# exp(-z) by ScalarE's Ln and Exp in place of VectorE's reciprocal, and another opening, in a fused attention and MLP kernel

## The reference

```
s = clip(hs @ Ws1.T @ Ws2.T + bs2, -32, 32)        # (B, H, T, M)
z = cumlogsumexp(s, axis=t);  es = exp(s);  enz = exp(-z)
A = tril(q @ k.T) * scale                           # q, k with rotary positions
ok = enz * (A @ es)
qv = softmax(ok)
W2 = tril((qv * enz) @ es.T)
o = rmsnorm(W2 @ v) * g_norm_weight * silu(g)
x = x + o @ Wo.T + mlp(hs)
```

## Time and profile before

| what | value |
|---|---|
| time, median of 3 runs | 1154.71 us (1154.1 to 1155.89) |
| profiled execution: time, span | 1155.05 us, 1153.3 us |
| busy TensorE | 1110.0 us, 96% of the span |
| busy VectorE | 950.5 us, 82% |
| busy ScalarE | 640.7 us, 56% |
| busy POOL | 422.4 us, 37% |
| mean granted TensorE clock | 0.986 |

### The profile page before, as it was taken

The page is one execution under the profiler, slowest core; times in us unless marked ns, Lnnn a source line. Parts: engine busy times, 40 slices in busy tenths (PEclk is TensorE's granted clock), DMA queues, the critical chain, the costliest instruction groups (busy, mean ns, idle before and its releaser), DMA issues.

```text
span 1153.3 us, 19874 instructions
## 1 busy us (share of the span) xinstructions
PE 1110.0 (96%) x6872; PEld 937.2 (81%) x6872; DVE 950.5 (82%) x1815; ACT 640.7 (56%) x1750; POOL 422.4 (37%) x307
## 2 busy tenths in 40 slices
PE   5789999999999999999999999999999999999995
PEld 4568888888888888888888888888888888888885
DVE  5978888788888889888887888878888888888863
ACT  4455456555645556554656655565564565655442
POOL 4323244422434335232453324443252434523131
PEclk9889999999999999999999999999999999999997
DMA  4002000020002000020000200001000100000001
GB/s 161 1 1 75 2 1 1 1 76 1 2 1 76 1 1 2 1 76 1 1 1 1 75 1 1 1 11 65 1 1 2 75 2 1 2 1 19 1 19 38
DMA packets 9124, 23.03 MB, mean 20 GB/s; under 512 B 832, under 2 KB 5824, under 8 KB 8000
## 3 DMA queue, kind: packets, MB, share of 16 engines
q1 hardware_dynamic: 9024, 21.76, 5.2%
HBM read 19.66 MB, written 2.10 MB: 19 GB/s over the span
## 4 chain that ended last, share of the span: by engine, by line
PE 82%; DVE 5%; issue 3%; ACT 2%; POOL 1%; POOLq 0%; DVEq 0%; ACTq 0%
PE bank L205 20%; PE bank L207 18%; PE bank L206 18%; PE bank L298 4%; PE bank L330 3%; PE bank L311 3%; PE bank L355 3%; PE bank L344 2%; PE bank L347 2%; PE bank L346 2%; PE bank L300 2%; DVE og L808 1%; PE bank L502 1%; PE bank L314 1%; PE bank L322 1%
## 5 line engine op out<-in xcount | busy, mean ns | idle before, releaser
L1165 POOL TENSOR_TENSOR inter_lo<-ffb,inter_hi 128x512 fp32r<-128x512 f32 x64 | 83.5, 1329 | 417.2 <-ACT inter_hi L650 417.2
L1156 POOL TENSOR_TENSOR qkT<-ra,xs 128x512 f32<-128x512 f32 x128 | 164.5, 1285 | 109.3 <-DVE xs L899 77.2
L619 ACT ACTIVATE sm<-bank,mx 128x64 f32<-128x64 f32 x256 | 76.5, 325 | 148.4 <-DVE mx L855 148.4
L896 DVE TENSOR_TENSOR ra<-bank,rope 128x512 f32<-128x512 f32 x128 | 87.8, 686 | 48.3 <-ACT xs L601 47.2
L844 DVE RECIPROCAL enzT<-enzT 128x256 f32<-128x256 f32 x64 | 111.6, 1744 | 0.0
L899 DVE TENSOR_TENSOR xs<-xs,rope 128x512 f32<-128x512 f32 x128 | 111.0, 867 | 0.0
L205 PE MATMUL bank<-xh,wqk_hi 128*128 128x512 f32 x256 | 110.7, 432 | 0.0
L205 PE MATMUL bank<-xh,wgu_hi 128*128 128x512 f32 x256 | 106.2, 415 | 0.0
L624 ACT ACTIVATE At<-bank 128x128 f32<-128x128 f32 x128 | 35.4, 276 | 126.7 <-DVE At L779 126.6
L207 PE MATMUL bank<-xh,wqk_lo 128*128 128x512 f32 x256 | 102.1, 399 | 0.0
L207 PE MATMUL bank<-xh,wgu_lo 128*128 128x512 f32 x256 | 101.5, 396 | 0.0
(11 more groups left out here) (146 smaller groups left out, 3171.6 us busy)
## 6 DMA issues: line engine op xcount, KB each, us to landing
raw<-in_w_qkvg SPq DMA_DIRECT2D x8, 1024.0 KB, 5.1
scaled<-in_w_scaled SPq DMA_DIRECT2D x8, 640.0 KB, 7.4
packed<-in_w_packed SPq DMA_DIRECT2D x8, 384.0 KB, 5.6
acc<-in_x SPq DMA_DIRECT2D x4, 512.0 KB, 8.0
out<-acc SPq DMA_DIRECT2D x3, 512.0 KB, 2.9
out<-acc SPq DMA_DIRECT2D x2, 256.0 KB, 2.1
ws_raw<-in_w_slot SPq DMA_DIRECT2D x8, 48.0 KB, 1.8
rope<-in_rope_tab SPq DMA_DIRECT2D x1, 256.0 KB, 5.8
```

Of the source, the lines that this page charges most:

```text
L619: ins = act.activation(sm[:, c], src[:, c], ACT.Exp, bias=mx[:, g:g + 1], accum_out=ssum[:, g:g + 1])
L896: dve.tensor_tensor(two(ra[i % 2][:, :]), two(pj[i][:, :]), cos, ALU.mult).then_inc(cos_done, 1)
L1156: pool.tensor_tensor(qkT[:, i, :], ra[i % 2][:, :], xs[i % 2][:, :], ALU.add).then_inc(roped, 1)
L1165: pool.tensor_tensor(inter[1][e][:, :], ffb[e][:, :], inter[0][e][:, :].bitcast(F32), ALU.subtract).then_inc(inter_lo, 1)
```

## The change

exp(-z) is now computed on ScalarE in two activations over all 512 tokens, Ln and then Exp with scale -1, and the reciprocals are gone from VectorE. The opening is ordered anew: 24 matmuls of the identity ahead of everything on TensorE (`WARM`), the VG weights loaded and split in two parts, other load order; VG projection ahead of the inner slot product; block 1's second half of x, its inner product and the slot scores moved into stage 0; and one block of x prepared in each of stages 0 (block 2) and 1 (block 3), where `prep` is set, through one PSUM bank (`sc[0]`). `normalise` is split into `x_stats` and `x_scale`. A new SBUF tile `xb` holds the scaled x of blocks 2 and 3, the Ws1 parts have tiles of their own, and the reserved DMA scratch is set to 1024.

```diff
@@ ScalarE
+            def invert(n, par):
+                act.wait_ge(scan_done, 2 * n + 2)
+                act.activation(enzT[par][:, :], enzT[par][:, :], ACT.Ln).then_inc(z_done, 1)
+                act.wait_ge(z_done, n + 1)
+                act.activation(enzT[par][:, :], enzT[par][:, :], ACT.Exp, scale=-1.0).then_inc(enz_ready, 1)
...
+                if first:
+                    copy_J(0, rg[0][:, :])
+                    invert(0, 0)
                 if not last:
                     slot_exp(st + 1, npar)
...
+                if prep:
+                    x_hi(prep, 0, sc[0])
+                    x_hi(prep, 1, sc[0])
                 if bp == 3 and more:
                     split_hi(hp + 1, W_QK)
                     prepare_scales(hp + 1)
...
+                else:
+                    invert(st + 1, npar)
                 softmax_exp(st)
@@ VectorE
-            def invert(n, par, b):
-                dve.wait_ge(scan_done, 2 * n + b + 1)
-                c = slice(b * T, (b + 1) * T)
-                dve.reciprocal(enzT[par][:, c], enzT[par][:, c]).then_inc(enz_ready, 1)
...
                 gate_arg(st, 1)
+                if prep:
+                    x_stats(prep)
...
                 hidden(st, 1)
+                if prep:
+                    x_scale(prep)
...
                 softmax_in(st, par)
-                if not last:
-                    invert(st + 1, npar, 0)
+                if prep:
+                    x_lo(prep, 0, sc[0])
                 softmax_max(st)
+                if prep:
+                    x_lo(prep, 1, sc[0])
...
                 if not last:
-                    invert(st + 1, npar, 1)
                     gate_g(st + 1, npar, 2)
@@ TensorE, opening
+            pe.wait_ge(ident_set, 1)
+            for i in range(WARM):
+                pe.matmul(pj[3][:, 0:P], ident[:, :], ident[:, :], start=True, stop=True)
+            for k in range(KT):
+                transpose_x(0, k, rg[k])
+            for i in range(NT):
...
             pe.wait_ge(ws1_lo, 1)
-            slot_inner(0, sc[0])
+            slot_inner(0, rg[0])
             project_qk(0, 0, 0, 0)
             project_qk(0, 0, 0, 1)
+            transpose_x(1, 0, rg[1])
             project_qk(0, 0, 0, 2)
-            slot_inner(1, rg[0])
             project_qk(0, 0, 0, 3)
@@ TensorE, stage
                 slot_reads(st)
+                if prep:
+                    pe.wait_ge(clip_done, st + 2)
+                    transpose_x(prep, 0, sc[0])
                 if not first:
                     outputs(st, 0, php, None)
                 if not last:
                     project_vg(st + 1, nbp, nhp, 2, True)
                 slot_rows(st)
+                if prep:
+                    x_split(KT * prep + 1)
+                    transpose_x(prep, 1, sc[0])
@@ POOL, opening
             x_pow(0)
+            pool.wait_ge(xn_done, 1)
+            for k in range(KT):
+                pool.wait_ge(w_hi if k else vg0_hi, 1)
+                pool.tensor_tensor(wvg[1][:, k, :], raw_k[:, k, 512:1024], wvg[0][:, k, :].bitcast(F32),
+                                   ALU.subtract).then_inc(w_lo if k else vg0_lo, 1)
+            split_lo(0, W_QK)
             pool.wait_ge(ws1_hi, 1)
...
+            dequantise(0, W_GU)
             x_pow(1)
-            split_lo(0, W_QK)
-            dequantise(0, W_GU)
```

More of the change, by code:

```diff
@@ L55 @@
 SLOT_K = 3 * GROUP
+WARM = 24
 W_VG, W_QK, W_GU, W_OD = range(4)
@@ L173, in build @@
         xn = [og[:, :].rearrange("p (n d) -> p n d", n=NT), G[1][:, :].rearrange("p (n d) -> p n d", n=NT),
[L174 removed]
+              xb[:, :, :], xb[:, :, :]]
         ws1 = osq[:, 0:KT * P].rearrange("p (k n) -> p k n", k=KT)
[L176 removed]
         xhl = (xh, xl)
@@ L495, in stage @@
                 pe.wait_ge(p_ready, st + 1)
[L496 to L499, removed]
+                if not first:
                     pe.wait_ge(acc_done, 2 * st - 1)
@@ L505, in stage @@
                     project_qk(st + 1, nbp, nhp, 0)
+                if prep:
+                    slot_inner(prep, sc[0])
+                if not last:
                     project_qk(st + 1, nbp, nhp, 1)
@@ L527, in stage @@
                 pe.wait_ge(v_ready, 4 * st + 4)
-                if first:
-                    slot_inner(3, rg[1])
-                else:
+                if not first:
                     pe.wait_ge(acc_done, 2 * st)
                 values(st, bp, 0)
[L533 to L536, removed]
+                if not last:
                     pe.wait_ge(J_ready, st + 2)
@@ L650, in hidden_hi, with x_hi @@
                 act.activation(inter[0][e][:, :], ffb[e][:, :], ACT.Copy).then_inc(inter_hi, 1)
[L652 to L655, removed]
+            def x_hi(bp, k, src):
+                act.wait_ge(xT_full, KT * bp + k + 1)
+                act.activation(xh[:, k, tokens(bp)], src[:, :], ACT.Copy).then_inc(xh_done, 1)
             def inner_copy(bp, src):
@@ L667, in _ @@
             ins.then_inc(ws1_hi, 1)
[L668 to L673, removed]
             prepare_scales(0)
@@ L698, in stage @@
                 more = hp < HP - 1
+                prep = st + 2 if st < 2 else None
+                if first:
+                    gate_square(st, 0)
                 off_diagonal(*a_args, 0, SCALE)
                 off_diagonal(*a_args, 1, SCALE)
-                gate_square(st, 0)
+                if not first:
+                    gate_square(st, 0)
                 gate_tanh(st, 0)
+                if first:
+                    slot_exp(0, 0)
+                    inner_copy(1, rg[1])
                 if bp == 1:
@@ L737, in stage @@
                     swap_halves(st + 1, 0)
+                if prep:
+                    inner_copy(prep, sc[0])
+                if not last:
                     swap_halves(st + 1, 1)
@@ L747, in stage @@
                     swap_halves(st + 1, 2)
-                if first:
-                    x_hi(3)
                 off_diagonal(*w_args, 2, 1.0)
@@ L1000, in stage @@
                 if first:
-                    invert(0, 0, 1)
-                if not first:
+                    gate_gelu(st, 0)
+                    inner_lo(1, rg[1])
+                else:
                     gate_scale(st)
@@ L1205, in stage @@
                 more = hp < HP - 1
+                if not first:
+                    norm_pow(st)
                 if first:
                     x_pow(2)
-                else:
-                    norm_pow(st)
                 if bp == 1:
```

254 lines of the change are left out of this document (130 added, 124 removed).

## The result

The changed kernel takes 1171.59 us (median of four runs, 1170.55 to 1173.59), the kernel before 1155.2 on the same occasions (four runs, 1154.1 to 1155.89). The ratio is 1.0144, 95% interval 1.0132 to 1.0155: slower by 1.4%, or by 16.4 us. 1180 was forecast, with 1157 to 1200 as the range. The profiled execution took 1171.61 us with a span of 1169.9, 16.6 above that of before.

What follows compares the result with a forecast made beforehand. TensorE, busy 1110.0 of 1153.3 us, was taken as the bound. Turns with clock falls 22.0, opening -7.5 and stage 1 +11.1 sum to +25.6; 1155.05 + 25.6 - 0.34 gives 1180 us, range 1157 to 1200.

Steps and rivals of the forecast that it cites:

- The turns: Seven turn stages (bp 3): the call makes the softmax 2.74 us late, TensorE waits 1.93 each, 13.5 us in all.
- The clock after such a wait: After the turns' TensorE waits: clock falls five times of seven, costing 8.5 us, bounds 0 and 11.9.
- likeliest range: Range of the likeliest case: 1164 us (no falls, opening 5 better) to 1190 (all falls, opening 6 worse).
- Ordinary stages: 22 ordinary stages: the call fits in ScalarE's wait for the maximum, ending 2.0 us before the softmax; cost 0.
- The opening: Start to stage 1's scores: scores start at 78.3 instead of 85.79, gain 7.5 us, bounds 2 and 13.
- The walk: Step-by-step timing of the new opening from row durations, from x's scaling at 7.95 to stage 1's scores at 78.3.
- The gap near 22: Opening: TensorE idles 6.7 us before block 1's transposes, waiting for x scaled behind decode, gates and a POOL-held sine product.
- Stage 1: Stage 1 now prepares block 3's x: idles of 2.4 and 2.7 us, two clock falls; cost 11.1, bounds 7 and 13.
- The end: The end of the kernel: claimed to be untouched by the change, with no term in the sum.
- A switch costs twice its row: Rival: table switches cost double, a call takes 6.5 us, turns wait 4.5 each; +54.7, 1209 us, chance 0.12.
- The loads cost nothing: Rival: both loads run in waits, a call takes 1.3 us, turns lose nothing; -3.3, 1151 us, chance 0.11.
- The turns absorb the call: Rival: ScalarE's lateness in the turns is caught up, only the opening counts; +3.6, 1158 us, chance 0.08.

Runs made afterwards that it cites:

- e2_call_alone: The kernel before with only exp(-z) changed: Ln and Exp on ScalarE ahead of the softmax, no reciprocals on VectorE; 1167.16 us, ratio 1.0094.
- e3_no_loads: The changed kernel with Copy in place of Ln, leaving one table load in the trace; 1151.65 us, ratio 0.996.
- e4_turns: The changed kernel with the exp(-z) call moved ahead of prepare_out in the seven turn stages; 1158.76 us, ratio 1.0028.
- e9_longer_wait: The changed kernel with one more 512-column copy on ScalarE ahead of the call in each turn stage; 1187.79 us, one run.
- e1_opening_alone: The changed kernel with exp(-z) back on VectorE as two reciprocals a stage; 1153.7 us, ratio 0.9987.
- e10_opening_dve: The same opening as e7_opening, but with exp(-z) by VectorE's reciprocals; 1147.66 us, ratio 0.9933.
- e7_opening: The changed kernel, call ahead of prepare_out (turns) and second x copy (stages 0, 1), opening reordered to scale block 1's x earlier; 1146.43 us, ratio 0.9922.

## Why the prediction was right, and where it was off

The forecast difference was 25.6 us, the measured one 16.4. The measured time lies well inside the range, but most of the distance is one term.

**The turns: right.** Predicted 1.93 us of lateness seven times, 13.5 in all; measured 1.92 a stage, 13.4 over the seven. The softmax was to be 2.74 late and is 2.65. e2_call_alone shows that the call alone does it, e3_no_loads that its loads do, e4_turns that its place does. The call, predicted at 3.9, delays the softmax by 3.78.

**The clock after such a wait: the step that failed.** "1.93 lies between; I take five falls of seven: 8.5 us" became no fall of seven and 0 us, the lower bound I had named. The lateness of 1.93 shows as an idle of 1.70, closer to the 1.43 of the earlier trace rows that had kept 1.00 than to the 2.59 that had not. In e9_longer_wait idles of 2.20 to 2.22 us brought a fall six times in seven, at 1.6 us each. Without that term the sum is 1171.8, 0.2 from the measured median, and a difference of 17.1 against 16.4. Part of this closeness is chance, since the errors of the opening (1.1), of stage 1 (0.2) and of the end (-1.5), below, nearly cancel. The lower end of the likeliest range, 1164, comes out only if the two falls of stage 1 (3.4) are left out as well; with them it is 1166.8, and both came.

**Ordinary stages: cost 0, right.** ScalarE in stage 2, before:

```profile
138.91 0.32 ACT L619 ACTIVATE sm<-bank,mx 128x64 f32<-128x64 f32 x1 [5.76 <-DVE mx L855]
```

and in the changed kernel:

```profile
138.01 1.28 ACT L625 ACT_TABLE_LOAD   x1
139.70 0.64 ACT L625 ACTIVATE enzT<-enzT 128x512 f32<-128x512 f32 x1 [0.40 <-DVE enzT L870]
...
143.76 0.32 ACT L641 ACTIVATE sm<-bank,mx 128x64 f32<-128x64 f32 x1 [1.48 <-DVE mx L882]
```

The first load runs while ScalarE would have waited for the scan, as predicted, and 1.48 us of the 5.76 are left. The prediction had 2.0 of the 6.33 of stage 1. In all 22 ordinary stages some wait is left, 1.48 to 2.44 us.

**The opening: -6.4 instead of -7.5.** The walk held step for step. TensorE in the opening of the changed kernel:

```profile
11.90 0.47 PE L209 MATMUL bank<-wvg_hi,xh 128*128 128x512 f32 x1 [0.98 <-DVE xl L974]
28.77 1.12 PE L414 MATMUL bank<-ident,G 128*128 128x128 f32 x4 [6.34 <-DVE G L968]
52.52 0.72 PE L414 MATMUL bank<-ident,xb 128*128 128x128 f32 x4 [2.33 <-DVE xb L968]
56.30 0.66 PE L331 MATMUL bank<-ident,okz 128*128 128x128 f32 x4 [1.67 <-DVE okz L877]
64.60 1.11 PE L518 MATMUL bank<-ident,sm 128*128 128x128 f32 x4 [5.55 <-ACT sm L641]
```

Predicted starts were 11.9, 28.5 (after 6.7), 51.7 (after 2.4), 55.65 and 63.65 (after 5.6). The walk is 0.3 short at 28.77, 0.8 at 52.52, and 1.1 at the start of stage 1 (79.37 against 78.3). The gap near 22 came about as said. VectorE, then POOL, in that opening:

```profile
12.90 3.04 DVE L937 SCALAR_TENSOR_TENSOR codes<-packed 128x768 int32<-128x768 int32 x1
...
26.40 2.31 DVE L968 TENSOR_SCALAR G<-acc,mv,rstd 128x256 f32<-128x256 f32 x4
...
12.59 2.53 POOL L1168 TENSOR_TENSOR wqk_lo<-raw,wqk_hi 128x1024 fp32r<-128x1024 f32 x1 [0.42 <-ACT wqk_hi L583]
```

The decode pass that begins while POOL splits takes 3.04 us and ends 0.8 after POOL (15.94 against 15.12). This is what the prediction took from the earlier trace rows.

**Stage 1: +11.3 instead of +11.1.** TensorE in stage 1 of the changed kernel:

```profile
95.78 1.10 PE L414 MATMUL bank<-ident,xb 128*128 128x128 f32 x4 [2.32 <-DVE xb L968]
...
110.06 1.12 PE L518 MATMUL bank<-ident,sm 128*128 128x128 f32 x4 [2.73 <-ACT sm L641]
```

Idles of 2.32 and 2.73 were forecast as 2.4 and 2.7.

**The end: -1.5, "untouched" in the prediction.** Its work is the same, and so are its longest waits (3.67 and 2.48 us), but TensorE stood at half clock there for 6.8 us, against 15.0 before. In the twelve profiled executions of this case, all with the same last stage, its length goes with that time: 45.8 us where it is 6.8, 46.1 to 46.8 where it is 10.2, 47.3 to 48.3 where it is 15 to 19. The long ones are before, e1_opening_alone, e2_call_alone, e9_longer_wait and e10_opening_dve, which no single edit sets apart. I take it for scatter, which was not tested.

**The rivals.** *A switch costs twice its row* is refuted: the Ln starts 0.02 us after its load has ended, and the next load 0.01 after the Ln. *The loads cost nothing* is refuted in the turns, and e3_no_loads shows what it would have given: 1151.65, where the prediction had said 1151. *The turns absorb the call* is refuted by the seven waits for sm in the turns, of which before had none.

The Trainium skill, "ScalarE: Activation LUTs", section "What ACT_TABLE_LOAD costs", states 1283 ns for a load, which 64 of 64 rows agree with, and 1380 ns of draining on top, which no row here shows: two switches and two activations fit into 3.78 us. The section "Table sets: the hidden batching unit" of the same page says that Ln and then Exp need one load, since one set holds both; in this kernel both had one in front of them every time. A build that keeps both in one set was not tried, and what it would give is open.

## What to carry to other kernels

A call that costs nothing in 22 stages of 32 lost 13.4 us in seven stages of another kind, because the slack ahead of the softmax was about 6 us in the ones (5.76 to 6.36) and 1.1 in the others: read the slack in every kind of stage, not in the mean. Work moved onto an engine belongs into a wait which that engine has anyway, so look for the instruction in front of it that waits (here `prepare_out` for POOL, and the second copy of x for TensorE); moving two lines was worth 20 us. And taking 111 us off an engine that hardly anybody waits for is worth little: 1.4 us ahead of stage 1 in e2_call_alone, where the clock had a part too, and nothing that can be told between e7_opening and e10_opening_dve.

## What the runs showed of the hardware that I had not expected

- The clock stayed at 1.00 after 28 idles of 1.67 to 1.70 us in four kernels, each in an otherwise full stretch, and fell to 0.50 for about 3.4 us after six of seven idles of 2.20 to 2.22 us. Half a microsecond more of waiting thus cost 2.1 us a stage. But the same wait of 2.32 to 2.33 us in stage 1 brought a fall in six profiled executions and none in four.
- A VectorE pass over 128x768 integers took 3.04 us beside POOL's split. The same pass takes 1.70 to 1.71 in seven later stages, beside a POOL addition of 1.27 us, and 0.94 in the opening of before, with no POOL instruction beside it. The Trainium skill, "SBUF — State Buffer", section "Who interferes with whom", says that a VectorE instruction with two SBUF inputs contends with a POOL instruction that reads SBUF, that VectorE's two-port modes do too, and that whoever issues first blocks the other for its whole instruction; the trace agrees, with an end 0.8 us after POOL's.
